# A Mamba scan in a decoder block: GpSimd multiplies three of the sixteen states by their C rows

## The reference, cut to what matters

```python
dA = jnp.exp(jnp.einsum('bdl,dn->lbdn', delta, A))          # A = -exp(A_log)
dBu = jnp.einsum('bdl,bnl,bdl->lbdn', delta, Bm, x)
C_t = jnp.transpose(Cm, (2, 0, 1))
def step(h, inp):
    dA_t, dBu_t, c_t = inp
    h = dA_t * h + dBu_t
    y = jnp.einsum('bdn,bn->bd', h, c_t)
    return (h, y)
```

## Time and profile before

| | |
|---|---|
| median of 3 runs | 2150.67 us |
| the profiled execution | 2149.31 us, of which the span of the trace is 2147.6 us |
| mean granted TensorE clock | 0.866 of full speed |
| busy shares | TensorE 75%, VectorE 66%, ScalarE 39%, GpSimd 30% |
| VectorE, scans (L992) | 128 instructions, 292.1 us |
| VectorE, products with C (L1001) | 128 instructions, 156.3 us |
| GpSimd, products with B (L968) | 128 instructions, 302.1 us |

### The profile page before, as it was taken

The page is one execution under the profiler, slowest core; times in us unless marked ns, Lnnn a source line. Parts: engine busy times, 40 slices in busy tenths (PEclk is TensorE's granted clock), DMA queues, the critical chain, the costliest instruction groups (busy, mean ns, idle before and its releaser), DMA issues. The chain is left out here.

```text
span 2147.6 us, 19868 instructions
## 1 busy us (share of the span) xinstructions
PE 1607.7 (75%) x6786; PEld 768.3 (36%) x6786; DVE 1416.9 (66%) x2091; ACT 827.5 (39%) x1552; POOL 640.9 (30%) x396
## 2 busy tenths in 40 slices
PE   4887699774977898739867997646679984488976
PEld 2454223242543222315432332212322222467753
DVE  6996878277987775659968873779687835221225
ACT  4542166543422566244422664433115661111210
POOL 2763311206655021136532112076340112100041
PEclk9899699986997899959987998789879996799975
DMA  5821720021006220030035200210062100466631
GB/s 178 289 70 47 157 38 1 1 79 45 1 0 167 38 38 1 0 123 1 0 95 109 38 2 0 82 37 0 5 156 41 21 1 9 153 200 196 198 98 61
DMA packets 125101, 149.27 MB, mean 70 GB/s; under 512 B 16000, under 2 KB 107784, under 8 KB 122952
## 3 DMA queue, kind: packets, MB, share of 16 engines
q1 hardware_dynamic: 121928, 139.61, 23.9%
q0 software_dynamic: 3072, 8.39, 1.2%
HBM read 96.47 MB, written 51.09 MB: 69 GB/s over the span
## 5 line engine op out<-in xcount | busy, mean ns | idle before, releaser
L165 PE MATMUL PS<-arena 128*32 128x512 f32 (+11 forms) x4126 | 883.4, 454 | 122.2 <-DMA arena<-in_ew 25.4
L165 PEld LDWEIGHTS PS<-arena 128*32 128x32 f32 (+3 forms) x4126 | 367.1, 128 | 615.8 <-ACT arena L1338 276.5
L1338 ACT ACTIVATE arena<-PS 128x512 f32<-128x512 f32 (+3 forms) x768 | 375.4, 541 | 378.3 <-PE PS L165 377.1
L968 POOL TENSOR_TENSOR arena<-arena 128x1024 f32<-128x1024 f32 x128 | 302.1, 2362 | 186.5 <-DVE arena L992 147.0
L1358 DVE TENSOR_REDUCE maxs<-PS 128x1 f32<-128x1024 f32 x256 | 302.3, 1217 | 78.4 <-PE PS L165 78.3
L992 DVE TENSOR_TENSOR_SCAN arena<-PS,arena 128x1024 f32<-128x1024 f32 x128 | 292.1, 2282 | 9.3 <-POOL arena L968 9.3
L948 ACT ACTIVATE PS<-arena,A_neg 128x511 f32<-128x511 f32 x256 | 166.0, 681 | 261.3 <-DVE arena L992 193.1
L165 PE MATMUL PS<-arena,ident 128*128 128x512 f32 (+1 forms) x560 | 259.8, 590 | 5.4 <-DVE arena L1001 5.4
L1191 POOL TENSOR_TENSOR arena<-xn 128x512 f32<-128x512 f32 x16 | 20.3, 1267 | 585.4 <-ACT xn L1326 585.4
L165 PE MATMUL PS<-bc,bc_sel 96*128 96x512 bf16 x128 | 52.3, 408 | 149.2 <-DVE arena L1001 98.1
L1001 DVE TENSOR_TENSOR arena<-arena,PS 128x1024 f32<-128x1024 f32 x128 | 156.3, 1221 | 7.1 <-PE PS L165 3.0
(11 more groups left out here) (251 smaller groups left out, 1807.8 us busy)
## 6 DMA issues: line engine op xcount, KB each, us to landing
arena<-in_ew SPq DMA_DIRECT2D x46, 512.0 KB, 5.2
arena<-stack_parts SPq DMA_DIRECT2D x288, 64.0 KB, 3.7
rows_in<-nil SPq DMA_DIRECT2D x17, 1024.0 KB, 11.2
arena<-b_rows SPq DMA_DIRECT2D x16, 1024.0 KB, 7.7
stack_parts<-arena SPq DMA_DIRECT2D x40, 384.0 KB, 3.1
arena<-stack_parts SPq DMA_DIRECT2D x96, 128.0 KB, 4.6
arena<-rows_in SPq DMA_DIRECT2D x23, 256.0 KB, 2.9
rows_out<-arena SPq DMA_DIRECT2D x23, 256.0 KB, 2.1
```

What stands on the lines that cost most here:

```text
L165: return nc.tensor.matmul(o, l, r, start=start, stop=stop)
L968: nc.gpsimd.tensor_tensor(b_sb[i % 2], u[:, 2 * kh:2 * kh + 2, :], Brow[:, n, :].unsqueeze(1).to_broadcast([P, 2, T]), ALU.mult).then_inc( ...
L1338: nc.scalar.activation(probs[(HG * s + h) % NPR][:, 0:N], bank(4 + n % 2)[:, 0:N], ACT.Exp, scale=HD ** -0.5).then_inc(S["ring_read"], 1)
```

## The change

In units whose state n is 5, 9 or 13 (POOL_C; six of the 32 units of a sample, 24 in all) GpSimd makes the product with C instead of VectorE. GpSimd cannot use the copy of C in PSUM bank 6, so three rows of C come by DMA, like those of B: b_src and b_rows hold 32 rows instead of 16, and one more DMA spreads three of them to all partitions (Crow). There are three buffers h_sb instead of two, and scan i waits for product i-3, no longer for product i-2. TensorE waits for the product of a unit at the semaphore of the engine that makes it, and leaves out the C rows of the three states.

GpSimd's product of unit g follows its product with B of unit g+2:

```diff
+                        if i >= 2 and pooled(UNITS[i - 2][1]):
+                            g = i - 2
+                            c = POOL_C.index(UNITS[g][1])
+                            if by_pool(g) == 0:
+                                pool.wait_ge(S["crow_in"], 16)
+                            pool.wait_ge(S["y_mm"], g - 1)
+                            nc.gpsimd.tensor_tensor(g_sb[g % 2], h_sb[g % 3],
+                                                    Crow[:, c, :].unsqueeze(1).to_broadcast([P, 2, T]),
+                                                    ALU.mult).then_inc(S["g_pool"], 1)
```

TensorE's loop over the units:

```diff
+            def product_done(eng, i):
+                if pooled(UNITS[i][1]):
+                    eng.wait_ge(S["g_pool"], by_pool(i + 1))
+                else:
+                    eng.wait_ge(S["g_done"], by_vector(i + 1))
...
-                        pe.wait_ge(S["g_done"], i + 1)
-                        if i + 1 < len(UNITS):
-                            row(UNITS[i + 1][1], 6, "cn_mm")
+                        product_done(pe, i)
+                        for later in range(i + 1, min(i + 3, len(UNITS))):
+                            if not pooled(UNITS[i][1]) and not pooled(UNITS[later][1]):
+                                row(UNITS[later][1], 6, "cn_mm")
+                                break
```

VectorE's loop:

```diff
-                        if i >= 2:
-                            dve.wait_ge(S["g_done"], i - 1)
-                        nc.vector.tensor_tensor_scan(h_sb[i % 2].rearrange(flat), decay(i).rearrange(flat),
+                        if i >= 3:
+                            product_done(dve, i - 3)
+                        nc.vector.tensor_tensor_scan(h_sb[i % 3].rearrange(flat), decay(i).rearrange(flat),
...
+                        if pooled(n):
+                            continue
                         dve.wait_ge(S["h_done"], i + 1)
-                        dve.wait_ge(S["cn_mm"], i + 1)
+                        dve.wait_ge(S["cn_mm"], by_vector(i + 1))
```

The rows of C:

```diff
+POOL_C = range(5, 14, 4)
...
+        ar_start(NAR - len(POOL_C) * T - 2 * T)
+        h_sb.append(half())
+        Crow = ar(len(POOL_C) * T).rearrange("p (n t) -> p n t", n=len(POOL_C))
...
+                        sp.dma_start(Crow, b_rows[NS + POOL_C.start:NS + POOL_C.stop:POOL_C.step, :]
+                                     .partition_broadcast(P)).then_inc(S["crow_in"], 16)
```

More of the change, by code:

```diff
@@ L42 @@
 K_PART = [0, 1, 2, 0, 1, 0]
+POOL_C = range(5, 14, 4)
 def decoder(nc, w, x_in, ctx_t, out):
     qkv_dram = nc.dram_tensor("stack_parts", (4, 3, H, HD, TC), BF16).ap()
-    b_rows = nc.dram_tensor("b_rows", (NS, T), F32).ap()
+    b_rows = nc.dram_tensor("b_rows", (2 * NS, T), F32).ap()
     rows_in = nc.dram_tensor("rows_in", (ROWS, DM), F32).ap()
@@ L122, in decoder @@
         bcr = sb("bcr", [2 * NS, 2, T])
-        b_src = sb("b_src", [NS, T])
+        b_src = sb("b_src", [2 * NS, T])
         maxs = sb("maxs", [P, 2, TT, 2 * HG])
@@ L294, in decoder @@
             bc3_ready dt_mm abs_done sp_ready cn_mm gen_in pow_mm pow_ev b_src_ready b_stored b_ready a_done
-            h_done g_done y_mm y_read gated outproj_mm bp_added qkv_mm hi_f_ready mid_ready parts_ready v_mm
+            h_done g_done g_pool crow_in y_mm y_read gated outproj_mm bp_added qkv_mm hi_f_ready mid_ready parts_ready v_mm
             v_init v_ready ones_ready max_mm max_done mt_mm mt_read mparts_ready ring_mm ring_read pv_mm
@@ L614, in _ @@
                         nc.scalar.activation(dtin[:], bank(0)[0:RK], ACT.Copy).then_inc(S["dtin_ready"], 1)
-                        nc.scalar.activation(b_src[:], bank(0)[RK:RK + NS], ACT.Copy).then_inc(S["b_src_ready"], 1)
+                        nc.scalar.activation(b_src[:], bank(0)[RK:RK + 2 * NS], ACT.Copy).then_inc(S["b_src_ready"], 1)
                         nc.scalar.activation(bc3[0:2 * NS], bank(0)[RK:RK + 2 * NS], ACT.Copy).then_inc(S["bc_hi"], 1)
@@ L834, in powers_out, with pooled, by_vector, by_pool @@
                 return sum(power_out(i) for i in range(s))
+            def pooled(n):
+                return n in POOL_C
+            def by_vector(i):
+                return sum(not pooled(n) for _, n in UNITS[:i])
+            def by_pool(i):
+                return sum(pooled(n) for _, n in UNITS[:i])
+            def product_done(eng, i):
[3 more added lines that the diff above has]
+                    eng.wait_ge(S["g_done"], by_vector(i + 1))
             def decay(i):
@@ L996, in _ @@
                             gate_channels(kh - 1)
+                        if pooled(n):
+                            continue
                         dve.wait_ge(S["h_done"], i + 1)
-                        dve.wait_ge(S["cn_mm"], i + 1)
+                        dve.wait_ge(S["cn_mm"], by_vector(i + 1))
                         if i >= 2:
                             dve.wait_ge(S["y_mm"], i - 1)
-                        nc.vector.tensor_tensor(g_sb[i % 2], h_sb[i % 2], bank(6).unsqueeze(1).to_broadcast([P, 2, T]),
+                        nc.vector.tensor_tensor(g_sb[i % 2], h_sb[i % 3], bank(6).unsqueeze(1).to_broadcast([P, 2, T]),
                                                 ALU.mult).then_inc(S["g_done"], 1)
```

## The result

| | before | changed |
|---|---|---|
| median | 2150.53 us (4 runs, 2150.28 to 2151.87) | 2209.64 us (4 runs, 2205.07 to 2212.65) |
| ratio | 1 | 1.0272, 95% interval 1.0253 to 1.029 |
| the profiled execution's span | 2147.6 us | 2206.9 us |
| mean granted TensorE clock | 0.866 | 0.854 |

The change makes the kernel 2.7% slower, 59 us. The forecast was 2208 us.

The account below looks back on a forecast made before the run. VectorE was taken to pace all four scan stages. Power steps with small terms 8.3 plus clock 6.7 gave 15.0 for each of three samples, 45; the fourth 13.5; +58 on 2150.67 gave 2208.7, stated as 2208, range 2174 to 2226.

Parts of the forecast that it names:

- VectorE's own gain: 24 products leave VectorE at 1.14 us each, 27.4 us in all; the rival that it comes through had 0.05.
- The chain of a group: Scan 5 to scan 9: product 7 starts at 9.40 after waiting 1.4 us; the group costs +0.17 us at full clock.
- The pair of products: GpSimd's product with B for unit 7, then unit 5's with C, back to back: 2.38 us each, done at 7.12.
- Power steps: First three samples: steps between pooled units' y matmuls and the next C row add 8.24 us per sample.
- small terms: Added to the power steps' 8.24 us per sample: -0.92 for absorbed waits and 6 x 0.17 for the groups, giving 8.3.
- clock term of 6.7: First three samples: groups behind units 20, 24 and 28 at the low clock, about 2.4 + 2.4 + 1.9 us per sample.
- -0.92: Per sample of the first three: today's waits of 0.23 and 0.69 us at products 14 and 15 are absorbed.
- The clock: TensorE idles 4.96 us, restarts at the low clock: 2.1 us per fourth-sample group; about 15 of 24 groups low.
- the 1.4 + 0.44 of the forecast: Product 7, first three samples: 1.4 us wait at full clock plus 0.44 for a turn behind unit 5.
- the rival that puts all 24 groups at the low clock: Clock falls also behind 3.0 us idle and less: +70 to +73 us, 2222 us; chance 0.10.
- Costs set at nothing: DMA of C hidden by 20 us; L983 beside GpSimd taken as 0, with up to 1.5 us per sample possible.
- The sum of 58: Whole kernel: 45 us for the first three samples and 13.5 for the fourth, together +58.5, used as 58.

Follow-up runs that it names:

- e5: Changed kernel plus 18 unread matmuls on TensorE ahead of each wait for GpSimd, fourth sample only; 1.0237 of the kernel before, fourth stage 120.7 us.
- e4: Changed kernel, but TensorE adds each pooled unit's product to y one unit later, from a buffer of its own; 0.9971 of the kernel before.
- e2: Changed kernel with all products that count on VectorE; GpSimd still makes the 24 products, into an unread buffer; 0.9995 of the kernel before.
- e7: Changed kernel, but GpSimd makes its product with C for one of two channel tiles only; 1.0095 of the kernel before, 2157.19 us.
- e3: Changed kernel, but in pooled units TensorE does the power step ahead of its wait for GpSimd's product; 1.013 of the kernel before.
- e0: The changed kernel run once more, same code, on another chip; 1.0295 of the kernel before, 2196.33 us.
- e1: Changed kernel with all products with C back on VectorE, keeping third buffer, wider b_rows and DMA of C; 0.9996 of the kernel before.
- e6: Changed kernel with states 3, 7, 11 on GpSimd instead, their products added to y two units later from their own buffer; 0.9901 of the kernel before.

## Why the prediction was right, point by point

- **What bounds the kernel, and what goes.** As forecast, the four scan stages hold it: 60.0 us, where the span grew by 59.3. VectorE's own gain is there as busy time, 31 us in the stages.
- **The chain of a group** (GpSimd's two products, y matmuls, row, product). Forecast for the low clock was product 7 at 9.40 + 1.92 = 11.3 us after scan 5; it was 11.36. Without the low clock the wait was forecast at 1.4 us; e5 shows 1.46. The pair of products was sized a little long: 2.30 us apart (1481.29 to 1483.59), not 2.38, so TensorE began at 7.06, not 7.20. That the start of product 7 fits so well is in part luck: the y matmuls held TensorE for 3.58 us, not 3.42, which makes up for it.
- **Who waits.** e4 shows that the place of the wait in TensorE's order is the cause, e2 that GpSimd's load is not, and e7 that its duration counts in full once TensorE waits.
- **Power steps.** Priced at 8.3 us a sample with the small terms; together with the clock term of 6.7 that was 15.0 for the first three stages, and 15.4 to 16.8 were measured. e3 takes 10 to 13 us of it away, against the stages of the first chip. The split between step and clock inside these stages was not measured by itself, since e3 removes both. The waits of 3.62 to 3.64 us of product 11, at full clock, are the 1.46 of e5 and the 2.17 of the power step to within 0.02 us. Of the small terms, -0.92 was too much: product 14 still waits 0.27 us, and products 8, 12 and 28 now wait 0.2 to 0.6 us, which the forecast did not have.
- **The clock.** 2.1 us for such a group of the fourth stage, 13.5 for the stage; measured 12.4, and 11.5 of these go when TensorE is kept busy for all but 0.95 us of each gap (e5). The low clock was forecast for units 21, 25 and 29, at full clock for 5, 9 and 13 with "3.0 us or less" idle. Unit 5 was wrong: after 2.90 us idle its y matmuls took 2.69 us in the first stage and 3.41 in the second, and product 7 waited 3.23 us and 3.33 us, not the 1.4 + 0.44 of the forecast. Only the first stages of e0 and e5 had it at full clock, with a wait of 1.89 us. Units 9 and 13 (1.64 and 0.78 us idle) were at full clock, so the rival that puts all 24 groups at the low clock is out. The first stage grew by 1.4 us more than the second, 1.3 of it because product 23 waited 6.12 instead of 4.86 us.
- **Costs set at nothing.** DMA of C: 13.3 to 14.9 us to landing, longer than the 4.4 to 11.5 of the earlier trace rows, and still 20 us early; with the buffers 0 by e1. L983 took 1.58 us in the middle of the first three stages, as before. In the fourth it took 1.33 us, where it had taken 2.19: `gate_channels` started later there, and GpSimd's product with B beside it ended sooner after L983 began. That is 0.9 us of the 1.1 by which the fourth stage grew less than forecast.
- **Where luck helped.** Outside the stages the trace shows +3.8 us in the parts between them and -4.3 after the last, which cancel; neither was forecast and neither has a cause that I tested. The sum of 58 has a high term (fourth stage, 1.1 us) beside a low one (first three, 2.6 us together). And the clock term of the first three stages came out right by two errors. Set against the waits at full clock (1.46 us, and 1.73 more for the power step ahead of products 23 and 27; 1.89 for product 7), the low clock cost products 23, 27 and 31 about 1.7 us each in the second and third stages, where 2.4, 2.4 and 1.9 were forecast, and product 7 about 1.4, where nothing was. That is 6.4 us beside the 6.7 forecast.

## What to carry to other kernels

What moved work costs is decided by the place where the next engine's program order waits for it: the same 24 products on GpSimd cost 59 us in the changed kernel, nothing in e2, and gave 6 us in e4. Look at what stands behind that wait, and who needs it; only there does the duration of the work count. Let the consumer take the slow engine's result later than it needs it, from a buffer of its own, and keep such results away from the end of an accumulation. On TensorE an idle gap can be paid a second time: after 4.81 us idle the next matmuls ran at the low clock and took 3.78 us instead of 1.88. So put independent work in front of the wait, not behind it.

## What the runs showed of the hardware that was not expected

- After the same idle time TensorE did not always restart alike. The first three samples of the changed kernel, e0 and e5 have identical code, and TensorE idles 2.89 to 2.91 us ahead of unit 5 in all nine of these stages. Its y matmuls then ran at full clock in two of them, with a wait of product 7 of 1.89 us, and at the low clock for a part or all of their time in the others, with waits of 3.23 to 4.31 us. Unit 21 (product 23), after 4.17 us idle, was followed by waits from 4.86 to 6.23 us. Stages of identical code therefore took 134.4, 135.1 and 137.7 us (the first), and 136.0 to 139.0 (the second and third). Nothing in these runs tells what decides it. Nor do they show that such gaps widen the spread from run to run: four runs of the changed kernel spread over 7.6 us on the first chip and 2.2 us on that of e0, and the kernel before over 1.6 us in four runs on the first chip and 7.6 us in the 22 on that of e1.

Unit 5 in the first and in the second stage of e0_changed_again, from TensorE's timeline:

```profile
81.72 1.98 PE L166 MATMUL PS<-arena,ident 128*128 128x512 f32 x4 [2.89 <-POOL arena L1000]
548.22 3.78 PE L166 MATMUL PS<-arena,ident 128*128 128x512 f32 x4 [2.89 <-POOL arena L1000]
```

Even a gap of 1.57 us can do it, though after 1.64 us ahead of unit 9 the changed kernel kept its full clock. In e3 a turn of four small transposes stands ahead of the wait at unit 5, with 0.69 us of idle time in front of it. The second and the third stage differ all the same:

```profile
538.61 1.98 PE L166 MATMUL PS<-arena,ident 128*128 128x512 f32 x4 [1.56 <-POOL arena L1003]
995.96 3.43 PE L166 MATMUL PS<-arena,ident 128*128 128x512 f32 x4 [1.57 <-POOL arena L1003]
```

This is what the second stage of e0_changed_again shows of VectorE's product 23, in its timeline, beside 4.86 us for the same product in the changed kernel's second stage:

```profile
623.39 1.22 DVE L1035 TENSOR_TENSOR arena<-arena,PS 128x1024 f32<-128x1024 f32 x1 [6.23 <-PE PS L166]
```

- A scan that follows another scan starts 2.18 us after it (two in 4.46 us), a little before the 2.28 us of a single one are over, so taking the product from between them saved 1.28 us (3.46 less 2.18) and not the 1.14 of the forecast. e6 keeps this gain: 24 x 1.28 = 31 us, less the waits that stay, is the source of the 17.0 us that its stages are shorter.
- VectorE's multiply L983, with both inputs in SBUF, took the longer the more of a GpSimd product ran beside it: 2.19, 1.58, 1.33 and 0.83 us in stages where they overlapped, and 0.69 in e4, where GpSimd was idle. VectorE's scans and products, with one input in PSUM, took 2.28 and 1.22 us beside GpSimd in every kernel.
